# A sort of edges by source: where in a chunk's 16 groups of ranks its reverse scans and the packing of its columns stand

## What is computed

```python
edge_index = jnp.stack([src, dst])
x = _layernorm(x + _L0_gnn_ref(x, edge_index, ...))            # hypergraph convolution, twice
x = _layernorm(x + _L1_gnn_ref(x, edge_attr_64, src, dst, ...)) # segment softmax by dst
x = _layernorm(x + _L2_gnn_ref(x, edge_index, ...))            # cosine similarity, summed by src
x = _layernorm(x + _L3_gnn_ref(src, dst, x, edge_attr_3, ...)) # segment softmax by dst
```

```python
e   = B_inv[:, None] * segment_sum(xt[node_idx], edge_idx, ...)
out = D_inv[:, None] * segment_sum(e[edge_idx], node_idx, ...)
```

## Time and profile before

| | |
|---|---|
| runs | 21825.98, 21826.02, 21843.0 us (median 21826.02) |
| profiled execution | 21834.51 us, span 21832.8 us |
| mean granted TensorE clock | 0.555 |
| busy share of the span | GpSimd 55%, VectorE 47%, ScalarE 21%, TensorE 20% |
| fill sort, about 3,490 to 7,485 us | 26 chunks, 1,664 indirect DMAs |

### The profile page before, as it was taken

How to read it: one execution, slowest core, us unless ns; L and a number is a source line. 1 busy time by engine, 2 the same in 40 slices (tenths; PEclk the granted TensorE clock), 3 DMA queues, 4 the chain that set the end, 5 groups by cost and what they waited for, 6 DMA issues and landing times. The chain is left out here.

```text
span 21832.8 us, 104239 instructions
## 1 busy us (share of the span) xinstructions
PE 4275.1 (20%) x22758; PEld 3247.4 (15%) x22758; DVE 10276.4 (47%) x18332; ACT 4673.7 (21%) x4961; POOL 12097.6 (55%) x12292
## 2 busy tenths in 40 slices
PE   1222224444434211111111111111111111100000
PEld 1111113333333210000000011111110000000000
DVE  4444445444444443333222235555555555567776
ACT  0100111111111002222233324333311111124442
POOL 4444443344343337776766655555555555467776
PEclk7555556766667655555555555555555555555555
DMA  2111111111111331111111113222222222234443
GB/s 63 37 37 36 35 41 50 46 39 47 39 48 43 121 141 53 53 52 52 48 53 54 52 56 94 94 94 94 91 62 65 64 64 64 57 108 141 141 141 111
DMA packets 583064, 1517.57 MB, mean 70 GB/s; under 512 B 276152, under 2 KB 276685, under 8 KB 539138
## 3 DMA queue, kind: packets, MB, share of 16 engines
q1 hardware_dynamic: 188414, 1028.89, 12.7%
q0 software_dynamic: 392160, 467.91, 9.9%
q10 hardware_dynamic: 2068, 16.12, 0.2%
HBM read 714.46 MB, written 803.57 MB: 70 GB/s over the span
## 5 line engine op out<-in xcount | busy, mean ns | idle before, releaser
L926 POOL DMA_INDIRECT rows<-tab,idx x6656 | 6650.0, 999 | 3734.1 <-issue 2170.6
L572 POOL DMA_INDIRECT moved_rows<-recs,sidx x1664 | 1619.0, 973 | 2361.9 <-DVE sidx L687 1863.5
L926 POOL DMA_INDIRECT rows<-in_x,idx x1664 | 1590.7, 956 | 1691.5 <-DMA idx<-src_d 1192.1
L926 POOL DMA_INDIRECT rows<-sums,idx x1664 | 1615.8, 971 | 722.5 <-issue 692.5
L1049 DVE TENSOR_REDUCE small<-SQ 128x16 f32<-128x1024 f32 x104 | 127.5, 1226 | 2929.9 <-ACT SQ L1032 1998.2
L989 PE MATMUL dist_ps<-dist_w,a3T 65*128 65x512 f32 x416 | 392.8, 1100 | 4463.9 <-issue 2694.3
L656 DVE CUSTOM_DVE_ANT_0 junk<-pV,ohh 128x98 f32<-128x98 f32 x1664 | 424.3, 255 | 1387.4 <-remote 1142.5
L2344 DVE TENSOR_TENSOR_SCAN own<-held,lastu,own 128x64 f32<-128x64 f32 (+1 forms) x1690 | 517.7, 341 | 951.5 <-issue 942.0
L321 DVE TENSOR_TENSOR oh_dl<-dig_dl,held 128x2048 bf16<-128x2048 uint16 (+1 forms) x104 | 237.6, 2285 | 1486.4 <-remote 994.2
L1773 PE MATMUL lg<-bd_fcr,attrT 128*128 128x128 f32 x1664 | 408.5, 421 | 2331.5 <-ACT attrT L1793 1477.4
L609 ACT ACTIVATE place<-pP 128x98 f32<-128x98 f32 x832 | 210.7, 253 | 2961.7 <-remote 1375.1
(11 more groups left out here) (462 smaller groups left out, 19874.2 us busy)
## 6 DMA issues: line engine op xcount, KB each, us to landing
sums<-DN SPq DMA_DIRECT2D x128, 1664.0 KB
rows<-tab,idx POOLq DMA_INDIRECT x6656
spread<-zeros SPq DMA_DIRECT2D x52, 1040.0 KB
own<-spread SPq DMA_DIRECT2D x26, 2080.0 KB
sums<-rows SPq DMA_DIRECT2D x26, 2048.0 KB
dists<-Y SPq DMA_DIRECT2D x104, 512.0 KB, 2.7
recs<-sums SPq DMA_DIRECT2D x26, 2048.0 KB, 16.5
sums<-OUT SPq DMA_DIRECT2D x26, 2048.0 KB
```

Source lines behind the costliest of these rows:

```text
L572: pool.indirect_dma_start(moved_rows if fill else rec, bass.IndirectOffsetOnAxis(ap=idx[b][:, j:j + 1], axis=0), recs[b][:, j, :], None).t ...
L926: pool.indirect_dma_start(rows[b][:, j, :], None, table, bass.IndirectOffsetOnAxis(ap=idx[b][:, j:j + 1], axis=0)).then_inc(rows_in[b], 16)
```

## The change

The bounds of the scans become GF = 1 and FE = 5: the 65 scans stand in the groups 1 to 4, sixteen or seventeen in a group, and the carry and `filled` follow in g = 4. `pack` stands at g = 1 instead of 12. In chunk 0 nothing moves: all scans stay at g = 2 and the packing at g = 0. The other call of `sort_edges`, without `fill`, keeps its packing at g = 12; it is in a branch that this run doesn't take.

```diff
-            GF = NGP // 2 - 2
+            GF, FE = 1, 5
...
-                        if g == (0 if zero(ch) else 3 * NGP // 4):
+                        if g == (0 if zero(ch) else GF if fill else 3 * NGP // 4):
                             pack(i, b)
...
-                        if fill and not zero(ch):
+                        if fill and not zero(ch) and GF <= g < FE:
                             fill_part(i, b, g)
                         if fill and zero(ch) and g == 2:
...
-                            for k in range(GF, NGP):
+                            for k in range(GF, FE):
                                 fill_part(i, b, k)
...
-                    if g >= GF:
-                        n = NGP - GF
-                        for f in range((F + 1) * (g - GF) // n, (F + 1) * (g - GF + 1) // n):
-                            v = ec[:, ::-1] if f == F else recs[b][:, ::-1, f]
-                            t = dve.tensor_tensor_scan(recs[b][:, ::-1, f], nxp[:, ::-1], v, after[:, f:f + 1],
-                                                       ALU.mult, ALU.add)
-                    if g == NGP - 1:
+                    n = FE - GF
+                    for f in range((F + 1) * (g - GF) // n, (F + 1) * (g - GF + 1) // n):
+                        v = ec[:, ::-1] if f == F else recs[b][:, ::-1, f]
+                        t = dve.tensor_tensor_scan(recs[b][:, ::-1, f], nxp[:, ::-1], v, after[:, f:f + 1],
+                                                   ALU.mult, ALU.add)
+                    if g == FE - 1:
                         t.then_inc(tail, 1)
```

## The result

The changed kernel took 21622.07 us (median of 4 runs, 21606.42 to 21624.93) beside 21834.51 us for the kernel before (median of 4): the ratio is 0.9901 with the 95% interval 0.9883 to 0.9918. It is faster by 212 us where 391 were forecast; the time lies in the forecast's range of 20950 to 21740. The profiled execution took 21624.93 us, its span is 21622.3 us.

What follows compares the result with a forecast made beforehand. Late TensorE signals during GpSimd's scatter were taken to bound the fill sort. Gains of 368 us (chunks 2 to 24) and 69.9 (end), less 46.4 (chunk 1), made 391.5, giving 21434 us, range 20950 to 21740.

Steps and rivals of the forecast that it cites:

- stall and turn: Fill sort, per chunk: time left after quiet groups and scans, to fall from 87.2 us to 67.9.
- chunk 1: Loses by having its own bursts in it: 87.6 us becomes 134.0, 46.4 us lost.
- at the end: Chunk 25 and its scatter: 223.9 us becomes 154, 69.9 us gained.
- the price of a burst: What 16 scatter DMAs cost the ranking: 14.4 us, the mean of 15.6, 10.5 and 17.2 read from chunk 0.
- Bursts joined without a pause: Sign in GpSimd's scatter that would show the forecast wrong and point to rival 1; pauses of 5 to 12 us were expected.
- theory A: From the experiments: a run of L us of indirect DMAs without a pause costs the ranking about L - 4 us.
- The turn: Fourth burst with the change to the next chunk: 20.7 us from chunk 0 plus 4 for a TensorE wait.
- Rival 1: Each scatter DMA costs the ranking the same wherever it stands; stall and turn stay 87.2 us, 21920 us; chance 0.10.
- Rival 2: VectorE slows GpSimd's DMAs: bursts grow by 5.4 us, 21970 us; chance 0.03.
- Rivals 3 and 4: 3: loop bursts cost 10.5 us, 20950 us, chance 0.09; 4: scatter stays late, 21910 us or nothing, chance 0.04.

Runs made afterwards that it cites:

- the kernel before, second trace: The kernel before, unchanged, profiled again on one chip beside the changed kernel and the one with sixteenths: 21805.9 us.
- the one with sixteenths: The changed kernel with a cast of 4 columns after every group and bursts of 4 DMAs: 21325.07 us held up, 16493.98 us where not.

## Why the prediction was right in its direction and nearly twice too large

- **The mechanism held.** Scatter in one piece, ranking held up for its length, gain by cutting the piece: stall and turn fell from 87.2 us a chunk to 145.0 - 56.5 - 13.6 = 74.9. The forecast was 67.9; the missing 7.0 us times 23 chunks are 161 us, 8.7 more are missing in chunk 1 and 7.1 at the end (7263.81 + 0.97 - 7103.69 = 161.1 where 154 stood in the sum). Together 177 of the 179 us that the gain fell short.
- **The failed step is the price of a burst, 14.4 us.** The changed kernel shows it alone between its third and fourth casts: 4779.25 - 4747.35 = 31.9 us in chunk 8, and 31.9 in the mean of the chunks 2 to 24, so 17.8 with 14.1 quiet. The two bursts between first and third cast cost 4747.35 - 4678.85 - 28.2 - 3.4 = 36.9, 18.4 each. In the second trace of the changed kernel, where it took 21577.66 us, a lone burst costs 17.0 in the mean and the pair 36.9, so the price moves by about 1 us between traces. I had taken chunk 0's quiet group of 4.12 us off its steps. But those 0.6 us a group are VectorE's second set of one-hots, which VectorE can do while it waits for a late signal; with 3.53 off each step, chunk 0 gives 18.0, 12.9 and 17.2 us, a mean of 16.0. That this is why the price was too low is argued from the sums, not shown by a run.
- **The joined bursts were not foreseen, and matter less.** "Bursts joined without a pause" was named as what would show the forecast wrong, though the sum had the second cast come three groups after the first burst's start, which is enough to see it. Against two lone bursts of 17.8 the pair costs 36.9 - 35.6 = 1.3 us more, and not the 4 that theory A gives to one more run. Likewise, in the 6 chunks of the profile that keep a pause of 1.6 to 2.4 us, first to third cast takes 67.6 us in the mean, in the 17 joined ones 68.5. So such a pause is worth 0.9 us, and most of the miss is the price of a lone burst.
- **The turn was put too high.** The sum added 4 us to chunk 0's 20.7, half of a wait of TensorE that nothing in the profile accounts for; no run shows that term. Fourth burst and turn are 4823.46 - 4779.25 - 14.1 - 10.2 = 19.9 us in chunk 9, 20.6 in the mean, where 24.7 stood. This gave 4.1 us a chunk back; the other three bursts took 11.2 more than forecast.
- **Rival 1, the conserved stall, was half of the truth.** In total the 64 DMAs cost 74.9 us where the forecast had 67.9 and the rival 87.2. On one chip, 86.3, 73.8 and 64.4 us for one, three and 4.9 runs in the mean say what is conserved and what isn't: an added run saved 6.2 us at first and some 5 later. Why the step from one run to three gives that much, when joining two bursts costs 1.3, isn't shown.
- **Rival 2 is out.** GpSimd's DMA took 973 ns in the mean before the change and 987 after it:

```profile
L572 POOL DMA_INDIRECT moved_rows<-recs,sidx x1664 | 1643.0, 987 | 2123.1 <-DVE sidx L687 837.2
```

  And the steps in chunk 8's joined run are (4727.69 - 4687.11) / 31 = 1.31 us, against 1.28. By the rule of the Trainium skill on the shared ports ("SBUF — State Buffer", "SBUF: two separate sides") GpSimd could have lost far more beside VectorE while that works in one of the modes that take the shared ports. Whether this kernel's instructions on VectorE do is shown by no run; the trace shows 0.03 us a DMA. The same section's statement that TensorE waits for nobody is about these ports. The prediction set it against the 20 us of late signals, which was a misreading: a signal that comes late is no wait for a port, and no run here bears on that statement.
- **Rivals 3 and 4 are out:** no burst cost 10.5 us in the loop, and the scatter does start after g = 4.
- **Not in the prediction at all:** that the stall isn't the program's own. With 84.8 us a chunk where the signals are prompt, the right forecast there would have been "no change". What makes the signals late on the one kind is open: nothing in the trace names it, and I had no kernel that switches it on or off. Three things narrow what can be said:
  - The ends of TensorE's matmuls are modelled in this profile. So "its signal comes late" can as well be a matmul that was done late; the traces don't tell the two apart, and the sums need only the delay.
  - The held-up traces have holes. Between 3700 and 7200 us of the kernel before, 60 of ScalarE's 715 copies of the histogram (L609) have no semaphore increment on record; between 2460 and 4320 us of the changed kernel where it isn't held up, none of 703. All 38 waits over 5 us that the profile gives TensorE's L758 as "issue" in the first stretch stand right behind such a copy. So they are waits for ScalarE, which itself had waited for TensorE, and no second delay.
  - Every execution on record has a span and a clock from the profiler. That the recording itself holds TensorE up on one kind, where its records are also the ones with holes, is a rival that no run here excludes.

## What to carry to other kernels

A wait whose releaser is "remote", behind an instruction of another engine that ended long ago, is a finding of its own: ask how it depends on what runs beside it before pricing anything else, and look whether it is there on another chip. A wait called "issue" in such a trace may only lack its releaser's record: look at what ended just before it. When a price is read from a stretch that differs from the target in anything else, take off the baseline of the path that waits, not that of the engine which can fill its own waits. And before a handover is moved, lay the releases and the lengths of what they release on one time axis: three groups of 3.5 us against a burst of 20 already say that the bursts join.

The version to keep of those run is the one with sixteenths: 0.9774 of the kernel before (0.9757 to 0.979) where the ranking is held up, against 0.9897 for the change, and 0.9994 (0.9984 to 1.0004) where it isn't.

## What the runs showed of the hardware

- The changed kernel, its DMAs issued in steps of 1.28 to 1.31 us in the mean on either kind, took 144 to 145 us a chunk on one kind of chip and 84.8 on the other. In the fill sort signals from TensorE were seen up to 47 us late on the one (the kernel before, second trace), and no late one on the other. Of the six groups of runs behind the forecast, five met the prompt kind, on four chips, and one the other.
- What a run of indirect DMAs cost the ranking grew about in step with its length: in the changed kernel a burst of 20 us cost 17.8 us and two of them joined 36.9. The kernel before paid 86 to 87 us for a run of 82, the turn included; the changed one, cut in three, 74 to 75.
- A pause of 1.3 us between runs of 4 and 8 DMAs was enough for one group of ranks to take 3.7 us, near its quiet 3.5; the next group, beside 8 DMAs, took 10.4.
